# A recurrent attention block on one core: key products from scaled weights with present and past input, and the receptance mix moved between the first scans

## What is computed

```
shifted = pad(x, one step)[:, :-1]                 # the input one time step earlier, zero at t = 0
xk = x * time_mix_k + shifted * (1 - time_mix_k)
xv = x * time_mix_v + shifted * (1 - time_mix_v)
xr = x * time_mix_r + shifted * (1 - time_mix_r)
k, v, r = xk @ Wk.T, xv @ Wv.T, xr @ Wr.T
# for each feature, over time, with w = -exp(time_decay), u = time_first:
#   mo = max(mx, k+u); out = (e^(mx-mo) num + e^(k+u-mo) v) / (e^(mx-mo) den + e^(k+u-mo))
#   ms = max(mx + w, k); num, den decay with e^(mx+w-ms) and take in e^(k-ms) v, e^(k-ms)
y = (sigmoid(r) * out) @ Wo.T
```

## Time and profile before

| | |
|---|---|
| median of 3 runs | 1348.11 us (1347.27 to 1349.8) |
| the profiled execution's own time | 1346.95 us |
| its span in the profile | 1344.9 us |
| mean granted TensorE clock | 0.972 |
| the stage around the change | from 1111.1 us of the span to 1182.8 us |
| busy in the whole span: PE, DVE, ACT, POOL | 1218.4, 969.6, 608.9, 516.1 us |

### The profile page before, as it was taken

How to read it: one execution, slowest core, us unless ns; L and a number is a source line. 1 busy time by engine, 2 the same in 40 slices (tenths; PEclk the granted TensorE clock), 3 DMA queues, 4 the chain that set the end, 5 groups by cost and what they waited for, 6 DMA issues and landing times. The chain is left out here.

```text
span 1344.9 us, 17092 instructions
## 1 busy us (share of the span) xinstructions
PE 1218.4 (91%) x5980; PEld 847.5 (63%) x5980; DVE 969.6 (72%) x1981; ACT 608.9 (45%) x1423; POOL 516.1 (38%) x424
## 2 busy tenths in 40 slices
PE   6988999999889889999799978999999978499997
PEld 2455556565567765333588847888888843168876
DVE  8878888887879987943544347888888868964355
ACT  3166666665565546345244424333333326143343
POOL 1068576675612222410263314444444410405420
PEclk9989999999999999999899989999999989799999
DMA  2122122111011113100645331100111000011101
GB/s 95 34 73 56 48 56 64 40 48 32 17 49 40 32 32 136 44 0 1 229 148 197 108 103 45 32 25 25 32 32 32 5 8 31 0 49 55 40 28 63
DMA packets 31508, 73.43 MB, mean 55 GB/s; under 512 B 5394, under 2 KB 15123, under 8 KB 28736
## 3 DMA queue, kind: packets, MB, share of 16 engines
q1 hardware_dynamic: 28848, 67.44, 16.3%
q0 software_dynamic: 1536, 3.86, 0.9%
q10 hardware_dynamic: 1040, 1.05, 0.2%
HBM read 55.89 MB, written 6.29 MB: 46 GB/s over the span
## 5 line engine op out<-in xcount | busy, mean ns | idle before, releaser
L179 POOL TENSOR_TENSOR sums<-scans 128x512 f32<-128x512 f32 x56 | 78.0, 1392 | 277.1 <-ACT terms L173 168.6
L637 ACT ACTIVATE probs<-ps_s,stats 128x256 f32<-128x256 f32 (+1 forms) x256 | 104.1, 419 | 58.8 <-DVE stats L734 57.3
L575 POOL TENSOR_TENSOR probs<-probs,stats 128x512 f32<-128x512 f32 x64 | 67.7, 1057 | 110.4 <-DVE stats L740 110.4
L199 DVE RECIPROCAL sums<-sums 128x256 f32<-128x256 f32 x56 | 98.1, 1752 | 1.8
L734 DVE CUSTOM_DVE_ANT_0 ps_s<-ps_s,mask 128x256 f32<-128x256 f32 (+1 forms) x256 | 82.9, 383 | 10.8 <-PE ps_s L875 10.5
L184 POOL TENSOR_TENSOR sums<-sums,terms 128x512 f32<-128x512 f32 x56 | 73.7, 1315 | 4.4
L2041 PE MATMUL K_ps_kvp<-K_wqkv_hi,K_xin_hi 128*128 128x256 f32 x256 | 74.7, 292 | 0.0
L1946 ACT ACTIVATE K_ks<-K_ps_kvp 128x256 f32<-128x256 f32 x64 | 24.5, 383 | 109.6 <-PE K_ps_kvp L2041 109.6
L1059 POOL TENSOR_TENSOR L3hid<-L3hid,L3sig 128x1024 f32<-128x1024 f32 x17 | 46.1, 2715 | 70.3 <-DVE L3hid L1185 37.8
L2041 PE MATMUL K_ps_kvp<-K_wqkv_lo,K_xin_hi 128*128 128x256 f32 x256 | 72.3, 282 | 0.0
L2041 PE MATMUL K_ps_kvp<-K_wqkv_hi,K_xin_lo 128*128 128x256 f32 x256 | 72.2, 282 | 0.0
(11 more groups left out here) (430 smaller groups left out, 3543.2 us busy)
## 6 DMA issues: line engine op xcount, KB each, us to landing
E_fc<-l_fc_dram SPq DMA_DIRECT2D x16, 1024.0 KB, 7.7
qswap<-qraw SPq DMA_DIRECT2D x60, 128.0 KB, 2.3
K_wqkv<-l_wqkv_dram SPq DMA_DIRECT2D x16, 384.0 KB, 3.2
L3wgu<-L_w_dram SPq DMA_DIRECT2D x17, 256.0 KB, 2.6
L0wgu<-L_w_dram SPq DMA_DIRECT2D x14, 256.0 KB, 2.6
L3wdn<-L_w_dram SPq DMA_DIRECT2D x17, 128.0 KB, 2.0
wkvq<-w_l0a_dram SPq DMA_DIRECT2D x4, 512.0 KB, 4.1
wo<-w_l0a_dram SPq DMA_DIRECT2D x4, 512.0 KB, 3.8
```

Source lines behind the costliest of these rows:

```text
L179: pstep.mark(pool.tensor_tensor(sums[:, k, :, :], scans[:, k, :, 0, :], scans[:, k, :, 1, :], ALU.add))
L199: dstep.mark(dve.reciprocal(den, den))
L575: pool.tensor_tensor(p1, p1, rs[:, 0:2].unsqueeze(2).to_broadcast([P, 2, T]), ALU.mult)
L637: ins = act.activation(dst[:, i % 2, :], src[:, i % 2, :], ACT.Exp, bias=stats[:, g % 4, 4 + i:5 + i], scale=-1.0, accum_out=stats[:, g % ...
```

## The change

It does four things, all in `stage_l3_attn`.

1. The key's mix leaves the input. ACT makes two scaled copies of the key's weights, `wk_now` (by mix) and `wk_past` (by 1 - mix), four instructions of 128x256 in all, and PE forms each key group from four products: two of `wk_now` with xin and two of `wk_past` with xin one step earlier (255 of each 256 columns). The two scaled copies of xin for k on ACT and the two mixes for k on DVE go away.
2. The load of the weights is two transfers: the key's 256 KB first, and the other 768 KB behind it.
3. On ACT the exponential of the decay, with its table load, comes ahead of the scaled copies for v and r; the copy `evac(0)` of the first key bank stands between v's scaled copies and r's. On DVE 1 - mix and the clearing come ahead of xin.
4. On DVE the mixes for v come first, then the scans of chunk 0's first two batches (which now wait for one key bank alone), then the mixes for r, then the scans of its last two batches. PE runs three unread products ahead in place of seven.

```
 @block.sync
-                sp.dma_start(w[:, :, :, :], io["l3_w"]).then_inc(s["ld_w"], 16)
+                sp.dma_start(w[:, 0, :, :], io["l3_w"][:, 0, :, :]).then_inc(s["ld_wk"], 16)
+                sp.dma_start(w[:, 1:4, :, :], io["l3_w"][:, 1:4, :, :]).then_inc(s["ld_w"], 16)
 @block.scalar
...
                 condition_act(act, sig)
-                act.wait_ge(xin_ready, 2 * l + 2)
-                for j, n in enumerate(("mk", "mv", "mr")):
-                    for ch in range(CH):
-                        act.activation(mixed[:, j, ch, :], xin[:, ch, :], ACT.Identity, scale=vec(n, ch)).then_inc(s["scaled"], 1)
+                act.wait_ge(s["rest_ready"], 1)
+                act.wait_ge(s["ld_wk"], 16)
+                for c in range(CH):
+                    act.activation(wk_now[:, c, :], w[:, 0, c, :], ACT.Identity, scale=vec("mk", c))
+                    ins = act.activation(wk_past[:, c, :], w[:, 0, c, :], ACT.Identity, scale=rest[:, c:c + 1])
+                ins.then_inc(s["wk_ready"], 1)
                 act.activation(rest[:, 6:8], vecs[:, VEC["decay"][0]:VEC["decay"][0] + 2], ACT.Exp).then_inc(s["w_exp"], 1)
+                act.wait_ge(xin_ready, 2 * l + 2)
+                for j, n in ((1, "mv"), (2, "mr")):
+                    for ch in range(CH):
+                        act.activation(mixed[:, j, ch, :], xin[:, ch, :], ACT.Identity, scale=vec(n, ch)).then_inc(s["scaled"], 1)
+                    if j == 1:
+                        evac(0)
...
-                for g in range(8):
+                for g in range(1, 8):
                     evac(g)
...
 @block.vector
-                condition_dve(dve, l, sig)
+                dve.tensor_scalar(rest[:, 0:6], vecs[:, VEC["mk"][0]:VEC["mk"][0] + 6], -1.0, 1.0,
+                                  ALU.mult, ALU.add).then_inc(s["rest_ready"], 1)
...
+                condition_dve(dve, l, sig)
...
+                mix(1)
                 dve.wait_ge(s["w_exp"], 1)
                 dstep.link(dve.tensor_scalar(rest[:, 6:8], rest[:, 6:8], -1.0, None, ALU.mult))
                 for ch in range(CH):
-                    dve.wait_ge(s["evac"], 2 * ch + 2)
...
                     for b in range(NB):
+                        if b % 2 == 0:
+                            dve.wait_ge(s["evac"], 2 * ch + b // 2 + 1)
+                        if (ch, b) == (0, 2):
+                            mix(2)
                         ins = dve.tensor_tensor_scan(top[:, ch, b, 1:T + 1], decayed.to_broadcast([P, T]),
...
 @block.tensor
-                unread_products(pe, ps[:, 7, :], 7)
+                unread_products(pe, ps[:, 7, :], 3)
+                pe.wait_ge(s["wk_ready"], 1)
+                waves = lambda x: x.rearrange("p (b t) -> p b t", b=2)
+                for g in range(4):
+                    m, h = g // 2, g % 2
+                    pe.wait_ge(xin_ready, 2 * l + 1 + h)
+                    for c in range(CH):
+                        pe.matmul(ps[:, g, :], wk_now[:, c, m * P:(m + 1) * P], xin[:, c, half(h)], start=(c == 0), stop=False)
+                    for c in range(CH):
+                        ins = pe.matmul(waves(ps[:, g, :])[:, :, 1:T], wk_past[:, c, m * P:(m + 1) * P],
+                                        waves(xin[:, c, half(h)])[:, :, 0:T - 1], start=False, stop=(c == CH - 1))
+                    ins.then_inc(s["done"], 1)
                 pe.wait_ge(s["ld_w"], 16)
-                for g in range(16):
+                for g in range(4, 16):
```

More of the change, by code:

```diff
@@ L2167, in stage_l3_attn @@
             mixed = sb("mixed", [P, 3, CH, NT])
+            wk_now, wk_past = sb("wk_now", [P, CH, C]), sb("wk_past", [P, CH, C])
             rest = sb("rest", [P, 8])
@@ L2176, in stage_l3_attn @@
             out1, out2 = sb("out1", [P, CH, NT]), sig
-            names = "ld_w w_exp scaled mixed done evac diff_ready exp_ready num_ready top_ready rwkv_ready".split()
+            names = "ld_w ld_wk rest_ready wk_ready w_exp scaled mixed done evac diff_ready exp_ready num_ready top_ready rwkv_ready".split()
             s = {n: sem("V_" + n) for n in names}
@@ L2201, in _ @@
             def _(act):
-                condition_act(act, sig)
-                act.wait_ge(xin_ready, 2 * l + 2)
-                for j, n in enumerate(("mk", "mv", "mr")):
-                    for ch in range(CH):
-                        act.activation(mixed[:, j, ch, :], xin[:, ch, :], ACT.Identity, scale=vec(n, ch)).then_inc(s["scaled"], 1)
-                act.activation(rest[:, 6:8], vecs[:, VEC["decay"][0]:VEC["decay"][0] + 2], ACT.Exp).then_inc(s["w_exp"], 1)
                 def evac(g):
@@ L2213, in evac @@
                         .then_inc(s["evac"], 1)
-                for g in range(8):
+                condition_act(act, sig)
+                act.wait_ge(s["rest_ready"], 1)
[4 more added lines that the diff above has]
+                ins.then_inc(s["wk_ready"], 1)
+                act.activation(rest[:, 6:8], vecs[:, VEC["decay"][0]:VEC["decay"][0] + 2], ACT.Exp).then_inc(s["w_exp"], 1)
+                act.wait_ge(xin_ready, 2 * l + 2)
[5 more added lines that the diff above has]
+                for g in range(1, 8):
                     evac(g)
@@ L2231, in _, with mix @@
                 dve.memset(den[:, :, :, 0:1], 0.0)
-                dstep.link(dve.tensor_scalar(rest[:, 0:6], vecs[:, VEC["mk"][0]:VEC["mk"][0] + 6], -1.0, 1.0, ALU.mult, ALU.add))
-                for j in range(3):
+                condition_dve(dve, l, sig)
+                dve.wait_ge(s["rest_ready"], 1)
+                def mix(j):
                     for ch in range(CH):
-                        dve.wait_ge(s["scaled"], 2 * j + ch + 1)
+                        dve.wait_ge(s["scaled"], 2 * (j - 1) + ch + 1)
                         m = wave(mixed[:, j, ch, :])[:, :, 1:T]
@@ L2288, in _ @@
             def _(pe):
-                unread_products(pe, ps[:, 7, :], 7)
+                unread_products(pe, ps[:, 7, :], 3)
[10 more added lines that the diff above has]
+                    ins.then_inc(s["done"], 1)
                 pe.wait_ge(s["ld_w"], 16)
-                for g in range(16):
+                for g in range(4, 16):
                     j, m, h = g // 4, g // 2 % 2, g % 2
                     if j < 3:
-                        pe.wait_ge(s["mixed"], j + 1)
+                        pe.wait_ge(s["mixed"], j)
                     else:
```

## The result

The changed kernel is slower: 1350.77 us against 1348.09 (medians of twelve runs each), ratio 1.0021 with a 95% interval of 1.0013 to 1.0029, so 2.8 us. One execution of the changed kernel took 2048 us at a granted clock of 0.556 and is left out of the ratio. The forecast was 1348.7 and no measurable change. The profiled execution took 1348.2 us, its span is 1346.2, its mean granted clock 0.974.

What follows compares the result with a forecast made beforehand. DVE's list was taken to bound the stage: removed work -2.41 us, new idle time +2.9 and small steps between shift L2251 by 0.63 us, so 1348.11+0.6 = 1348.7 us, range 1346.8 to 1350.9.

Steps and rivals of the forecast that it cites:

- DVE's list sets the stage's end: Stage of the change: DVE is busy nearly throughout, 31.75 of 33.00 us in one stretch, and the next stage starts when it ends.
- two mixes are worth 2.4 us: DVE's two mixes for k go, 2.41 us less; if DVE never waited longer, the gain would be 2.4 us.
- the landing: Key's 256 KB of weights on SP's queue: taken to land 2.6 us after issue, at 1113.7.
- the second issue costs nothing: The other 768 KB, issued 0.33 us later, land by 1116.4; v's products need them only at 1129.4.
- The 17 loads: Transfers of the key load's size in the trace: median 2.6 us to land, between 2.5 and 3.6.
- late weights alone: Rival: key weights land after 3.9 us without a clock fall, +1.3 us, 1350.0; chance 0.16 together with slow writes.
- F_w's 3.9: Load in the stage before, issued at the start of a stage like this load, which took 3.9 us to land.
- a landing over 3 us: Sign, for the key weights' load, that the forecast would be wrong; 2.6 us was assumed.
- Is all else ahead?: Check of ACT, PE and POOL after L2251: none becomes late, so the 0.6 us shift reaches the end.
- that rival, which was to carry the slower side: Clock falls in PE's 1.7 us gap before the key products: 2.15 us lost, 1350.9, or 1352.2 with late landing; chance 0.12.
- The chance of 0.83: Whole kernel: chance given to "same", within 2.7 us of 1348.11, beside faster 0.05 and slower 0.12.
- the mark: Start of DVE's instruction L2251 at 1126.51, whose shift is the end's shift; forecast 0.63 us later.

Runs made afterwards that it cites:

- b1: Changed kernel with the other weights' 768 KB issued only when the key's 256 KB have landed; 1.0012 of the kernel before.
- b2: Kernel before with one extra 128x1024 DVE instruction (a sum nobody reads) ahead of the first scan; 1.0012 of the kernel before.
- d3: Kernel before with two extra 128x1024 DVE instructions (sums nobody reads) ahead of the first scan; 1.0037 of the kernel before.
- a3: Changed kernel with no unread products ahead of the key groups in place of three; 1.0039 of the kernel before.
- a4: Changed kernel with r's mixes directly behind v's on DVE, and the first key bank's copy behind r's scaled copies on ACT; 1.0007 of the kernel before.
- c3: Changed kernel without the past-input products for k, so key groups have four instructions; 1.0004 of the kernel before.
- b4: Changed kernel with weights issued in the stage before, r's mixes behind v's, and the exponential with table load behind all scaled copies; 0.9983 of the kernel before.
- c2: Changed kernel with only its weights issued in the stage before; 1.0001 of the kernel before.
- c1: Changed kernel with r's mixes behind v's and the exponential with table load behind all scaled copies, weights loaded as there; 0.9996 of the kernel before.

## Why the prediction was wrong

**What held.** DVE's list sets the stage's end; two mixes are worth 2.4 us; DVE waits for v's first copy and then for the second key bank with r's mixes queued behind (3.84 and 1.32 us for 3.1 and 1.35). A scaled 128x256 copy took 0.49 to 0.51 us, a key group 3.43, a product with a shifted result 591 ns, beside 592 without, so the write to a shifted place is free. ACT, POOL and PE stayed ahead. The table load took its 1.28 us and no drain: the copy ahead of it ends at 1114.81, the load starts at 1114.83, the exponential at 1116.12. The Trainium skill ("ScalarE: Activation LUTs", What ACT_TABLE_LOAD costs) counts 2.66 us for a switch; the trace doesn't agree, after as before.

**The step that failed first** is the landing: "I take 2.6, the value of the many", and "the second issue costs nothing". The key's weights landed at 3.3 to 3.6 us. The 17 loads gave 2.5 to 3.6 us, and without 768 KB issued 0.38 us behind it this load took 2.8; I costed the second issue for v's products and not for what it does to the first. b1 gives back 0.5 us of it. This term makes the shift 1.3 us (1.3 to 1.5 in the five profiles) in place of 0.6. The rival "late weights alone" comes nearest to it, with about half of its 1.3 us and with another cause than F_w's 3.9, and "a landing over 3 us" was rightly named as a sign of being wrong.

**The step that failed second** is the end of "Is all else ahead?": "the shift of 0.6 us goes through to the end". It doesn't go through one to one. The next stage's router products ran into the lower clock that before had come just behind them, and took 0.7 to 0.9 us more. b2 and d3 show that lateness alone does this, as long as the clock falls at the same place; in a3 it didn't, and the router lost nothing. I had looked for the clock in the gap ahead of the key products, where it stayed at 1.00 with a gap of 2.3 us; that rival, which was to carry the slower side, is not the cause. The measured 1350.77 lies inside the stated range of 1346.8 to 1350.9, but that is luck: the upper end came from that rival, which did not occur.

**A third piece is read and not tested.** In all five profiles of the changed kernel PE, or its weight loads, is held once near the end, behind a late `L3wdn` load, and in none of the three of the kernel before; in the first it is about 0.7 us. Over all profiles the sum bears this out: with the router's excess taken off, the part behind the stage is 161.9 to 162.1 us in the ten without the hold, and 0.3 to 1.0 us more in the seven that have it and nothing else. Which transfer meets it, and why it shifted, stays open: a4 and c3 show it, while a2, with two unread products more than the changed kernel, a3, b1, b4 and c2 do not.

The sum in the first profile is then 1.3+0.7+0.7 = 2.7 us, beside 2.8 timed (1.8 to 3.9 by the interval). The two later timings of the changed kernel gave 2.2 and 1.6 us, with intervals that reach to 3.1 to 3.5; they don't contradict the sum, and don't sharpen it. The chance of 0.83 for no measurable change was too high because it counted only what happens inside the stage, with 0.6 us as its middle and the bound at 2.7.

**Where the 2.4 us went.** Two mixes fewer should have brought the mark 2.4 us forward; it came 1.26 us later, so 3.7 us were lost. The wait for the second bank takes 1.1 of them (a4: 16.61 to 15.49), waiting for the weights 1.5 (c2: 16.61 to 15.12), the table load ahead of v's copies 1.1 (a4 to c1: 15.49 to 14.42). Each can be removed, and b4 without all three has the mark at 12.77, 2.6 us ahead of the kernel before.

## What to carry to other kernels

Moving work off the busiest engine pays only when what it waits for comes earlier too: here two instructions fewer were paid for by later inputs and by a wait with ready work queued behind it. Put ready work ahead of a wait, issue small loads where nothing follows them closely, and place a table load where no one waits behind it. And price a shift of a stage's end with the clock of what comes next: where a fall of the clock lies just behind a run of products, a microsecond of lateness cost 1.5 to 1.7 here (b2, the changed kernel, d3). It is a price to look for, not a rule: in a3, 2.8 us late, the fall had moved and its profile shows nothing added.

## What the runs showed of the hardware

- A 256 KB load landed 3.3 to 3.6 us after its issue when 768 KB were issued 0.38 us behind it from the same queue (ten profiles), and 2.8 us when they were not (one profile).
- PE idle for 2.3 to 2.6 us (the changed kernel, a4) kept its clock at 1.00; idle for 3.05 us (c1, ahead of 1198.98) and for 5.5 us (a3) it came back at 0.50, and in a3 the first four products took 3.39 us in place of 1.98.
- The clock also fell from 1.00 to 0.50 with PE fully busy: within the 128x9 products in the changed kernel, and in a3 within 128x512 products, 1 us behind them. In 15 of 18 profiles it fell 79.4 to 79.9 us behind the stage's start, whether the router began 75.8 or 77.9 us behind it; in a3, b4 and c1 at 83.2, 76.6 and 86.7.
- Four scaled copies of 128x256 and a table load followed one another on ACT without a pause: copy to load 0.02 us, load 1.28 us, load to exponential 0.01 us.
